# Group norm and attention over rows: straight code, x from the image, statistics over more rows, one transposing DMA per row

## The reference

```python
g = x.reshape(16, 64, 256, 32, 4)                       # image, row, token, group, channel
gn = (g - mean(g, (1, 2, 4))) / sqrt(var(g, (1, 2, 4)) + 1e-5)
q, k, v = split(gn @ W_qkv.T + b_qkv)                   # per row: 2 heads of 64 channels
p = softmax(q @ k.T / sqrt(128))                        # 256 x 256 for each head
out = x + concat_heads(p @ v)
```

## Time and profile before

| | |
|---|---|
| time, median of 3 runs | 3886.53 us (3881.05 to 3887.36) |
| profiled execution, own time | 3887.38 us |
| its span, first to last instruction | 3885.6 us |
| busy: PE / DVE / ACT / POOL | 3790.3 / 3713.4 / 3081.1 / 2429.5 us |
| granted TensorE clock, mean | 0.997 |
| DMA moved | 809.15 MB, mean 208 GB/s |

### The profile page before, as it was taken

One profiled execution on the slowest core, in us unless ns is written; L12 is line 12 of the kernel. 1 busy time (PEld: TensorE's weight loads), 2 busy tenths in 40 slices (PEclk: granted clock), 3 DMA queues, 4 the chain that ended last, 5 costly groups with the idle time before them and its releaser, 6 DMA issues.

```text
span 3885.6 us, 144060 instructions
## 1 busy us (share of the span) xinstructions
PE 3790.3 (98%) x44133; PEld 2976.9 (77%) x44133; DVE 3713.4 (96%) x6114; ACT 3081.1 (79%) x8193; POOL 2429.5 (63%) x3089
## 2 busy tenths in 40 slices
PE   4999999999999999999999999999999999999998
PEld 3777777777777777777777777777777777777777
DVE  5999999999999999999999999999999999999998
ACT  2788878888788887878878788787888888888786
POOL 1657566575665656566575665756657566575787
PEclk9999999999999999999999999999999999999999
DMA  7999999999999999999999999999999999998988
GB/s 188 215 210 216 214 210 214 213 213 214 210 214 209 214 216 209 213 210 214 215 209 215 211 215 211 211 213 209 212 210 212 215 213 213 211 205 182 177 179 177
DMA packets 2441865, 809.15 MB, mean 208 GB/s; under 512 B 2179072, under 2 KB 2441600, under 8 KB 2441600
## 3 DMA queue, kind: packets, MB, share of 16 engines
q1 hardware_dynamic: 2311040, 679.97, 89.7%
q10 hardware_dynamic: 130560, 125.86, 11.8%
HBM read 134.42 MB, written 134.22 MB: 69 GB/s over the span
## 4 chain that ended last, share of the span: by engine, by line
PE 50%; DVE 29%; issue 12%; ACT 4%; POOL 2%; DVEq 2%; DMA 1%; SPq 0%; ACTq 0%; POOLq 0%
PE s_pair L298 14%; PE qk_bank L276 14%; PE o_bank L314 10%; DVE p_lo L437 10%; DVE neg_max L429 10%; PE v_bank L286 6%; DVE bn L461 4%; ACT prob L394 3%; PE xt_bank L268 3%; POOL p_hi L600 2%; PE v_bank L283 1%; DVE o_norm L456 1%; DVE rsum L449 1%; DVEq L461 1%; DVE v_lo L443 1%
## 5 line engine op out<-in xcount | busy, mean ns | idle before, releaser
L600 POOL TENSOR_SCALAR p_hi<-prob 128x1024 f16<-128x1024 f32 x1024 | 1072.7, 1048 | 1403.1 <-ACT prob L394 1105.4
L394 ACT ACTIVATE prob<-s_pair,neg_max 128x256 f32<-128x256 f32 x4096 | 1610.8, 482 | 256.2 <-DVE neg_max L429 115.3
L437 DVE SCALAR_TENSOR_TENSOR p_lo<-prob,p_hi 128x1024 f16<-128x1024 f32 x1024 | 1357.7, 1326 | 54.8 <-POOL p_hi L600 37.2
L429 DVE TENSOR_REDUCE neg_max<-s_pair 128x4 f32<-128x1024 f32 x1024 | 1238.6, 1210 | 16.0 <-PE s_pair L298 15.1
L374 ACT ACTIVATE qk<-qk_bank,b_in 128x256 f32<-128x256 f32 x2048 | 861.5, 472 | 482.0 <-PE qk_bank L276 476.1
L298 PE MATMUL s_pair<-qk 64*128 64x256 f32 x8192 | 1164.7, 403 | 1.2 <-ACT qk L374 1.0
L276 PE MATMUL qk_bank<-xc,w_norm 128*128 128x256 f32 x4096 | 1160.1, 406 | 0.0
L616 POOL TENSOR_TENSOR y_ring<-image,o_norm 128x256 f32<-128x256 f32 x1024 | 1042.5, 1018 | 4.4 <-DMA out_dram<-y_ring 3.0
L276 PEld LDWEIGHTS qk_bank<-xc,w_norm 128*128 128x128 f32 x4096 | 695.1, 189 | 393.1 <-issue 337.7
L314 PE MATMUL o_bank<-v_hi,pt_lo 128*128 128x65 f16 x8192 | 851.2, 193 | 37.4 <-issue 19.5
L298 PEld LDWEIGHTS s_pair<-qk 64*128 64x128 f32 x8192 | 707.1, 186 | 219.8 <-issue 171.9
(11 more groups left out here) (72 smaller groups left out, 2075.9 us busy)
## 6 DMA issues: line engine op xcount, KB each, us to landing
out_dram<-y_ring SPq DMA_DIRECT2D x512, 256.0 KB, 2.8
image<-in_x_dram ACTq DMA_DIRECT2D x480, 256.0 KB, 3.4
pt_hi<-p_hi SPq DMA_TRANSPOSE x1024, 3.8
pt_lo<-p_lo SPq DMA_TRANSPOSE x1024, 3.2
image<-in_x_dram SPq DMA_DIRECT2D x4, 2048.0 KB, 16.3
w_in<-in_L_conv_W_qkv_dram SPq DMA_DIRECT2D x1, 192.0 KB, 2.4
b_in<-in_L_conv_b_qkv_dram SPq DMA_DIRECT2D x3, 0.5 KB, 2.1
```

The lines of the kernel that those rows point to most:

```text
L394: ins = act.activation(prob[:, m, c:c + TOK], s_bank[m][h][:, a * TOK:(a + 1) * TOK], ACT.Exp, bias=neg_max[:, m, h, a:a + 1])
L429: dve.tensor_reduce(neg_max[:, m, :, :].rearrange("p h a -> p (h a)"), s_pair[m][:, :].rearrange("p (b k) -> p b k", b=HEADS * J), AX.X, A ...
L437: dve.scalar_tensor_tensor(out=p_lo[:, v % 2, :], in0=prob[:, v % 2, :], scalar=P_SCALE, in1=p_hi[:, v % 2, :], op0=ALU.mult, op1=ALU.subt ...
L600: pool.tensor_scalar(p_hi[:, v % 2, :], prob[:, v % 2, :], P_SCALE, 1.0, ALU.mult, ALU.mult).then_inc(phi_done, 1)
```

## The change

- All loops are unrolled: every engine's code is one straight list of steps, and all counts are constants.
- `x_ring` and `refill` go. PE transposes x straight from `image`.
- `p_hi` and `p_lo` become the two halves of one tensor `p_both`, `pt_hi` and `pt_lo` those of `pt_both`. SP issues one transposing DMA for a row (128 x 2048), when `p_low` of the row is done, in place of two of 128 x 1024. Its semaphore `both_in` takes the place of `hi_in` and `lo_in` in every wait: `p_high(v)`, `p_low(v)` and `values(v)`.
- The 32 `bn_stats` of an image are spread over 40 rows from row 8 on, the 23 short operations over rows 48 to 60, two or three in a row. So `LAG` falls from 20 to 8.

```diff
-    FINISH = 12
-    STATS_FROM = ROWS - FINISH - GROUPS
+    FINISH = 16
+    STATS_FROM = 8
...
-        x_ring = sb("x_ring", [P, 4, J * C])
...
-        p_hi = sb("p_hi", [P, 2, QK], F16)
-        p_lo = sb("p_lo", [P, 2, QK], F16)
-        pt_hi = sb("pt_hi", [P, 4, PAIR, P], F16)
-        pt_lo = sb("pt_lo", [P, 4, PAIR, P], F16)
+        p_both = sb("p_both", [P, 2, 2, QK], F16)
+        p_hi, p_lo = p_both[:, :, 0, :], p_both[:, :, 1, :]
+        pt_both = sb("pt_both", [P, 4, 2 * PAIR, P], F16)
+        pt_hi, pt_lo = pt_both[:, :, 0:PAIR, :], pt_both[:, :, PAIR:2 * PAIR, :]
...
-        STAT_MM_AT = (0, 2, 6)
-        STAT_OPS_AT = {0: ((1,),), 1: ((2,), (3,), (4,), (5,)), 2: ((6,), (7,)), 3: ((8, 9), (10,), (11,), (12,)),
-                       4: ((13,), (14,), (15,), (16,)), 5: ((17,), (18,), (19,), (20,)), 6: ((21,),),
-                       7: ((22,), (23,))}
+        STAT_MM_AT = (0, 4, 11)
+        STAT_OPS_AT = {0: ((1,),), 1: ((2,), (3,)), 2: ((4,), (5,)), 3: ((6,), (7,)), 5: ((8, 9), (10,)),
+                       6: ((11,), (12,)), 7: ((13,), (14,)), 8: ((15,), (16,)), 9: ((17,), (18,)),
+                       10: ((19,), (20,), (21,)), 12: ((22,), (23,))}
...
+            for i in range(-2 * UNROLL, BLOCKS + 2 * UNROLL):
+                step(i)
...
-            def transpose_high(base, v, at):
+            def transpose_both(base, v, at):
                 if not known_below(base, 4 - v):
                     wait_apart(sp, pv_done, base + (v - 3))
                 wait_apart(sp, phi_done, base + (v + 1))
-                sp.dma_start_transpose(pt_hi[:, v % 4, :, :], p_hi[:, v % 2, :]).then_inc(hi_in[v % 2], 16)
-
-            def transpose_low(base, v, at):
                 wait_apart(sp, plo_done, base + (v + 1))
-                sp.dma_start_transpose(pt_lo[:, v % 4, :, :], p_lo[:, v % 2, :]).then_inc(lo_in[v % 2], 16)
+                sp.dma_start_transpose(pt_both[:, v % 4, :, :],
+                                       p_both[:, v % 2, :, :].rearrange("p s k -> p (s k)")).then_inc(both_in[v % 2], 16)
...
-                run(-2, transpose_low)
+                run(-2, transpose_both)
                 run(-7, store)
-                run(-1, transpose_high)
...
-                m = v % 4
-                pe.wait_ge(ring_in, base + (v + 1))
+                par, row = at
...
-                    mm = pe.transpose(xt_bank[:, j * P:(j + 1) * P], x_ring[:, m, j * C:(j + 1) * C], ident[:, :])
+                    mm = pe.transpose(xt_bank[:, j * P:(j + 1) * P], image[:, par, row, j * C:(j + 1) * C], ident[:, :])
...
-                pe.wait_ge(hi_in[v % 2], landed(base, v))
-                pe.wait_ge(lo_in[v % 2], landed(base, v))
+                pe.wait_ge(both_in[v % 2], landed(base, v))
...
-                    dve.wait_ge(lo_in[v % 2], landed(base, v - 2))
+                    dve.wait_ge(both_in[v % 2], landed(base, v - 2))
...
             def p_high(base, v, at):
                 if not known_below(base, 2 - v):
-                    wait_apart(pool, hi_in[v % 2], landed(base, v - 2))
+                    wait_apart(pool, both_in[v % 2], landed(base, v - 2))
                     wait_apart(pool, plo_done, base + (v - 1))
...
-                run(+6, refill)
                 run(-4, finish)
```

More of the change, by code:

```diff
@@ L108, in groupnorm_attention @@
         loaded = [sem(f"loaded{i}") for i in range(2)]
-        ring_in = sem("ring_in")
         stored = [sem(f"stored{i}") for i in range(2)]
-        hi_in = [sem(f"hi_in{i}") for i in range(2)]
-        lo_in = [sem(f"lo_in{i}") for i in range(2)]
+        both_in = [sem(f"both_in{i}") for i in range(2)]
         xt_done = sem("xt_done")
@@ L138, in groupnorm_attention @@
         STAT_STEPS = 23
+        MEASURE_ROWS = ROWS - FINISH - STATS_FROM
         MEANS_READY, SQUARES_READY, RSTD_READY = 1, 7, 21
         STAT_AT = J * HEADS * (HC + 1)
-        STAT_MM_AT = (0, 2, 6)
-        STAT_OPS_AT = {0: ((1,),), 1: ((2,), (3,), (4,), (5,)), 2: ((6,), (7,)), 3: ((8, 9), (10,), (11,), (12,)),
-                       4: ((13,), (14,), (15,), (16,)), 5: ((17,), (18,), (19,), (20,)), 6: ((21,),),
-                       7: ((22,), (23,))}
+        STAT_MM_AT = (0, 4, 11)
+        STAT_OPS_AT = {0: ((1,),), 1: ((2,), (3,)), 2: ((4,), (5,)), 3: ((6,), (7,)), 5: ((8, 9), (10,)),
+                       6: ((11,), (12,)), 7: ((13,), (14,)), 8: ((15,), (16,)), 9: ((17,), (18,)),
+                       10: ((19,), (20,), (21,)), 12: ((22,), (23,))}
         block = ctx.enter_context(nc.Block())
@@ L160, in schedule, with step @@
         def schedule(eng, order, share=None, bring=None):
-            def step(base, first_row, u, par, row=None, what=None, coming=None):
-                def run(lead, stage, *head):
[L168 to L175, removed]
+            def step(i):
+                img, row = divmod(i, ROWS)
+                par = img % 2
+                what = coming = None
+                if 0 <= img < IMAGES - 1 and 0 <= row - STATS_FROM < MEASURE_ROWS:
+                    group = (row - STATS_FROM) * GROUPS // MEASURE_ROWS
+                    if group != (row - STATS_FROM - 1) * GROUPS // MEASURE_ROWS:
+                        what = (MEASURE, img + 1, group)
+                elif 0 <= img < IMAGES - 1 and row >= ROWS - FINISH:
+                    what = ("finish", img + 1, row - (ROWS - FINISH))
+                if 0 <= img < IMAGES - 1 and row < LAG:
+                    coming = (img + 1, 1 - par, ROWS - LAG + row)
+                elif 0 <= img < IMAGES - 2 and row >= LAG:
+                    coming = (img + 2, par, row - LAG)
+                def run(lead, stage, *head):
+                    v = i + lead
+                    if 0 <= v <= LAST:
+                        stage(*head, 0, v, (v // ROWS % 2, v % ROWS))
@@ L177, in next_image @@
                 def next_image(place):
                     if what is not None and (place == MEASURE) == (what[0] == MEASURE):
-                        share(base, u, par, what, place)
-                if coming is not None and u % LOAD_ROWS == 0 and bring is not None:
-                    bring(base, u, *coming)
-                order(run, next_image)
[L185 to L216, removed]
@@ L218, in schedule @@
-            run_image(0, 0, True, False)
-            for img in range(1, IMAGES):
-                run_image(img, img % 2, False, img == IMAGES - 1)
+                        share(0, i, par, what, place)
+                if bring is not None:
+                    if 0 <= i < 2 * UNROLL:
+                        for c in range(i, CHUNKS - LAG // LOAD_ROWS, 2 * UNROLL):
+                            bring(i, 1, 1, c * LOAD_ROWS)
+                    if coming is not None and row % LOAD_ROWS == 0:
+                        bring(i, *coming)
@@ L411, in order, with bring @@
                 run(0, v_high)
-            def bring(base, u, img, par, row, free=False):
-                if not (free or base is None or known_below(base, LAG)):
-                    act.wait_ge(y_done, base + (u + LOAD_ROWS - LAG))
+            def bring(i, img, par, row):
+                if i >= LAG:
+                    act.wait_ge(y_done, i + LOAD_ROWS - LAG)
                 rows = bass.ds(row, LOAD_ROWS)
@@ L565, in share @@
                 if what[0] == MEASURE:
-                    if u == 0:
+                    if what[2] == 0:
                         dve.wait_ge(loaded[1 - par], (what[1] - 1 + par) * (8 * CHUNKS)
@@ L601, in p_high @@
                                    ALU.mult).then_inc(phi_done, 1)
[L603 to L608, removed]
             def finish(base, v, at):
@@ L628, in _ @@
             pool.memset(half_ones[:, :], 2.0 / P).then_inc(const_done, 1)
-            pool.wait_ge(first_in[0], 16)
             def order(run, next_image):
                 run(0, p_high)
-                run(+6, refill)
                 run(-4, finish)
```

## The result

The changed kernel takes 4671.12 us (median of 4 runs, 4667.23 to 4679.57), the kernel before 3886.82 (4 runs, 3881.05 to 3887.36): a ratio of 1.2021 with a 95% interval of 1.2004 to 1.2039. Forecast were 4337 us, a ratio of 1.116. So the sign came out as forecast, and the size lies above the high end of the range (4540).

What follows compares the result with a forecast made beforehand. PE was taken to bound the kernel before, at 3.65 us a row. Start 53.9 + 57, rows with loads 3736, rows without 472 and end 17 gave a 4336 us span, so 4337 us; range 3990 to 4540.

Steps and rivals of the forecast that it cites:

- The loop: `p_high`, `p_low`, one double DMA and its landing in series before `p_high` two rows later: 8.33 us with loads, 7.93 without.
- terms 3 and 5: Hand-overs in the series: `p_low`'s end to DMA issue, 0.11 us; landing to the next `p_high`, 0.35 us.
- L with loads: Merged DMA's time from start of issue to landing in rows with loads and straight code: 5.04 us.
- The start: First row maximum at 53.9 us, then eight rows taking 57 us, as all loads of image 1 fall there.
- The step that failed: Instruction fetch in straight code delays the merged DMA's landing by 0.3 us, between 0 and 1.6, added to the loads' delay.
- term 2: End of `p_high` to end of `p_low`: 1.78 us, since without the copy y_ring goes first and delays `p_low`.
- The base of L: Merged DMA's landing without additions: twice the 1.24 us issue plus 1.86 us after it, 4.34 us.
- the share of the loads: Load traffic delays the merged DMA's landing by 0.4 us, between 0 and 1.5.
- the operations spread out over more rows: Spread `bn_stats` and short operations on DVE: 0 at rows of 4.17 us; at most 59 us gained if PE stays the bound.
- the tail: From the last row maximum to the end: 17 us, against 15.3 before, with the later landing.
- The long DMA is quick: Rival: merged DMA lands in under 4.0 us even with loads, PE stays the bound, 3845 us; chance 0.13.
- `p_low` goes first: Rival: `p_low` starts before y_ring, ending 1.42 us after `p_high`; rows of 3.99 us with loads, 4154 us; chance 0.13.

Runs made afterwards that it cites:

- e5: The kernel before with only the merged DMA of 128 x 2048 per row added; loops, copy and old statistics kept: 4275.42 us.
- e6: The changed kernel with each load from image 2 on cut to 16 of 256 values of a row and partition: 4447.84 us.
- e7: The changed kernel with `finish` of row i-4 on POOL also waiting for `p_low` of row i, so y_ring never runs beside it: 4509.11 us.
- e10: The kernel before with the merged DMA and straight code, keeping the copy `refill`, `LAG` 20 and old statistics places: 4572.13 us.
- e4: The changed kernel with three buffers instead of two in `p_both` and three semaphores for its DMA: 3981.34 us, ratio 1.0249 to the kernel before.
- e9: e5 with each load from image 2 on cut to 16 of 256 values of a row and partition: 4165.59 us.
- e1: The changed kernel with the merged DMA alone undone, two early transposing DMAs per row: 3869.38 us, ratio 0.9951 to the kernel before.

## Why the prediction was right in its mechanism and wrong in its size

**The loop.** That it closes in series held. That half of the sum of the five means is the pace (4.53 us for both in the changed kernel) proves nothing by itself: the terms run without a gap from one `p_high` to the next in the same buffer, so they add up to two rows whatever sets the pace. What shows the series is that terms 3 and 5 are no more than hand-overs: 0.10 and 0.38 in the median in the changed kernel, and the same in e5, e6, e7 and e10. In e4, with its third buffer, `p_high(v+2)` starts 1.0 us before that landing in the median. The terms, in us:

| term | forecast | changed kernel, mean |
|---|---|---|
| 1. `p_high` | 1.05 | 1.09 |
| 2. its end to the end of `p_low` | 1.78 | 1.95 |
| 3. to the issue | 0.11 | 0.11 |
| 4. L with loads | 5.04 | 5.54 |
| 5. landing to `p_high` | 0.35 | 0.38 |
| sum | 8.33 | 9.07 |

From row 8 to the last maximum 4660.9 - 101.0 = 4560 us went by, where 3736 + 472 = 4208 were forecast: +352. The start gave 9 back and its first maximum came 1 earlier; the span is 342 above the forecast one, so nothing else is missing.

**The step that failed** is what was added to L for straight code, "so +0.3, between 0 and 1.6", and that it was simply added to the loads' share. Of the 0.74 us by which the loop is longer than forecast, L is 0.50; the next is term 2 with 0.17. The base of L came out right, by luck (the last section says why): 4.34 forecast, and 4.29 in the mean in e5's last image, in a loop and without loads. So did the share of the loads: 0.4 forecast. The mean L, worked out from issues and landings in rows 8 to 47 of images 2 to 13, or of the last image for "no loads" (in e9, whose loads are cut, of images 2 to 13; straight code in e5 and e9 is rows 54 to 61):

| mean L, us | no loads | loads |
|---|---|---|
| loop (e5; no loads: last image) | 4.29 | 4.64 |
| loop (e9, loads cut) | 4.33 | |
| straight, in the same kernels (e9, e5) | 4.88 | 5.38 |
| straight (e10) | 4.80 | 5.49 |
| straight (changed kernel) | 4.86 | 5.58 |

Loads alone add 0.35. Straight code alone adds 0.51 (e10) or 0.55 (e9), and beside loads 0.74 (e5) or 0.85 (e10). I took +0.3 from a median in a stretch of 18 us, for a DMA of half the size; its maximum, 4.7, gave the 1.6, but my high end took only 0.5 of it. The loads' effect on top of straight code is larger than in a loop, 5.49 - 4.80 = 0.69.

That the cause is the fetch of instructions rests on sorting rows, not on an edit that takes away the fetch alone. e10's straight rows show 23 fetch blocks in 40 rows and e5's loop 3. I sorted the rows of images 1 to 15 by the packets that run in the first 4.2 us after the issue (shorter than any landing, so that a late DMA does not meet more of them):

- With no packet of a load or of either fetch queue, the DMA lands after 4.26 us in the mean in the changed kernel (76 rows), 4.27 in e10 (57), 4.26 in e5 (87) and 4.26 in e9 (201): the same in loops and in straight code.
- In e9, images 2 to 15, rows in the loop (8 to 47) land after 4.28 without a block of q8 and 5.01 with one, straight rows (54 to 61) after 4.41 and 5.16. The difference goes with the block, not with the kind of code.
- In the last image of the changed kernel, which loads nothing, 34 rows without a block of q8 take 4.30 and 30 rows with one 5.45: 1.15 in 30 of 64 rows is 0.54 a row, about all that straight code adds there.

A block of q8 is one packet, and it takes 0.95 us in the median. That the landing waits for the DMA engine that is busy with it is an inference from these numbers, not shown. Beside loads a part stays open: with a load, but no block at all between issue and landing, the mean is 5.06 in the changed kernel and 4.60 in e5.

The Trainium skill (Runtime: NRT & Kernel Launch, section Instruction fetch mechanics) says that instructions come in blocks of 16 KiB through a DMA queue of the engine's own, and that the cost is mostly hidden; it also says that kernels prefer full unrolling, since a taken branch can break the prefetch. The size of the blocks agrees for q8 (5.85 MB in 357); those of q14 are half as large (2.10 MB in 256). The page's advice holds with two early DMAs (e1, where unrolling is part of a gain of 0.5%) and fails with the merged one (e10: +297 us): here the fetch was not hidden from a transposing DMA on the critical path.

**Term 2** was forecast as 1.78 and has this as its median; the mean is 1.95. y_ring does go first, as forecast: in 603 of the 800 rows it is running when `p_low` starts, and `p_low` never goes first of the two (in the other rows they do not overlap). From the end of `p_high` to the start of `p_low` is 0.03 in the median, but 0.39 in the mean, since in 319 rows DVE is still in another operation. In e10, where the copy L578 stands between `p_high` and y_ring, `p_low` goes first in 468 rows and y_ring in 211, `p_low` takes 1.38 in the mean and the term is 1.76. So the removed copy did lengthen this term, by 0.19, and that step held. It is the largest difference between the loops of e10 and of the changed kernel (8.83 and 9.07), whose times differ by 4671 - 4572 = 99 us; e10 also has the old statistics, and these were not run apart from the copy.

**The rest.** That the operations spread out over more rows bring nothing while the loop sets the pace fits the 710.6 us that DVE waits for `p_high` in any case, but no run takes them apart. Term 5 and the tail held. The start was put 9 us too high; which of its terms, was not looked into.

**The rivals.** *The long DMA is quick* fell: L is never under 4.2, and had to be under 4.0. The estimate of 3.2 to 3.4 from the rates of the Trainium skill (DMA: Bandwidth & Descriptors, section Latency and other measured facts) is too low by 0.8 or more here. *`p_low` goes first* fell: y_ring does. That straight code or the statistics cost their time by themselves fell with e1. A lower clock is no rival either: the mean granted TensorE clock was 0.985 in the profiled run, 0.997 before, and PE holds 1% of the chain.

**Where the 784 us come from**, one edit at a time: merge alone 4275 - 3887 = +388; unrolled +297; the copy gone and statistics spread +99. Without the merge, the last two are together a gain (e1); in the loop that the merge left without slack they cost 396 us.

## What to carry to other kernels

Before two transfers are merged, write down the loop that each one closes through its buffers: a merge puts them in series, since the first part waits for the second and is released with it, and a saved issue is worth nothing against that. If such a loop is over the pace, another buffer frees it, but then look at the next reader of the same landing. Once a DMA sets the pace, price everything else that uses the DMA engines, instruction fetch too, by the mean of a stretch in which it happens in every row, and with the other traffic on; here the medians of quiet stretches came out too low, and the shares did not just add up.

## What was not expected of the hardware

The issue of the 128 x 2048 transposition takes 1.32 us at least (median 1.98), and not, as was forecast, twice the 1.24 of one of 128 x 1024. Yet it lands after 4.2 at least, where the small one takes 3.0. The 4.34 came out right, but from a reason that the trace does not bear out, since the length of the issue does not set the flow: issue ends early and the DMA goes on.

The fetch of instructions is 5.85 MB (q8) in the whole run, 0.5% of the DMA engines' time, and yet straight code goes with 0.5 to 0.85 us more on the mean landing. A queue's share of busy time did not tell how much later a transfer lands beside it.
